# Batch 0's second half on GpSimd, batch 1's projections one matmul at a time, and another order of spills and pads

## What is computed

```python
ys = y / sqrt(128); d = rsqrt(einsum('bi,io->bo', ys * ys, w * w) + 1e-8)
xc = einsum('bsi,io->bso', x * ys[:, None, :], w) * d[:, None, :]     # modulation
q, k, v = split(xc @ w_qkv.T); q, k = rope(q), rope(k)               # 16 heads of 8
attn = softmax(where(causal, q @ k.T / sqrt(8), -inf)) @ v
x = x + attn @ w_out.T
x = x + ffn(moe(x, cond))                                             # 8 experts, 8 zones
```

## Time and profile before

| | |
|---|---|
| median of 3 runs | 181.37 us (181.26 to 181.59) |
| profiled execution: time, span | 180.98 us, 179.1 us |
| PE busy | 168.9 us (94%) |
| DVE busy | 138.9 us (78%) |
| ACT busy | 134.3 us (75%) |
| POOL busy | 93.8 us (52%) |
| share of PE in the chain that ended last | 70% |
| DMA | 24.28 MB, mean 136 GB/s |

### The profile page before, as it was taken

The page is one execution under the profiler, slowest core; times in us unless marked ns, Lnnn a source line. Parts: engine busy times, 40 slices in busy tenths (PEclk is TensorE's granted clock), DMA queues, the critical chain, the costliest instruction groups (busy, mean ns, idle before and its releaser), DMA issues.

```text
span 179.1 us, 3278 instructions
## 1 busy us (share of the span) xinstructions
PE 168.9 (94%) x943; PEld 116.8 (65%) x944; DVE 138.9 (78%) x444; ACT 134.3 (75%) x224; POOL 93.8 (52%) x117
## 2 busy tenths in 40 slices
PE   6899999899999999988999999996999989999992
PEld 2656575565666666653758767864687867788881
DVE  5588989989898899980586999699799658637551
ACT  3569177688768888889734787953879999999970
POOL 5508088985463969688532522021769931676000
PEclk9999999999999999999999999999999999999999
DMA  4824775676686567520110899960760000001001
GB/s 144 294 46 107 191 203 159 218 234 213 166 267 208 143 194 194 164 94 5 62 51 17 231 345 344 347 178 4 241 230 0 0 4 0 0 2 59 0 4 59
DMA packets 15349, 24.28 MB, mean 136 GB/s; under 512 B 2844, under 2 KB 4828, under 8 KB 15308
## 3 DMA queue, kind: packets, MB, share of 16 engines
q1 hardware_dynamic: 14532, 23.29, 42.2%
q10 hardware_dynamic: 800, 0.79, 1.7%
HBM read 18.71 MB, written 5.27 MB: 134 GB/s over the span
## 4 chain that ended last, share of the span: by engine, by line
PE 70%; DVE 11%; ACT 7%; issue 6%; POOL 4%; DVEq 0%; ACTq 0%; POOLq 0%
PE psum L1407 11%; PE psum L1540 10%; PE psum L1541 9%; PE psum L1542 9%; PE psum L1467 8%; PE psum L1443 7%; PE psum L1286 3%; PE psum L1338 2%; PE psum L1352 2%; ACT t_probs L1105 2%; DVE psum L772 2%; DVE t_raw L924 1%; PE psum L1402 1%; ACT t_q_pad L1155 1%; PE psum L1447 1%
## 5 line engine op out<-in xcount | busy, mean ns | idle before, releaser
L772 DVE CUSTOM_DVE_ANT_0 psum<-psum,t_causal 128x128 f32<-128x128 f32 (+3 forms) x128 | 58.6, 525 | 5.8 <-PE psum L1407 3.0
L1105 ACT ACTIVATE t_probs<-psum 128x1024 f32<-128x1024 f32 (+2 forms) x48 | 40.9, 883 | 8.2 <-PE psum L1443 5.2
L1407 PE MATMUL psum<-t_stacked,t_q_pad 96*128 96x256 f32 (+2 forms) x104 | 33.3, 391 | 0.5 <-DVE t_row_max L772 0.2
L1407 PEld LDWEIGHTS psum<-t_stacked,t_q_pad 96*128 96x128 f32 x104 | 18.4, 189 | 12.4 <-DVE t_row_max L772 10.2
L672 POOL TENSOR_SCALAR_AFFINE_SELECT t_probs<-t_probs 128x512 f32<-128x512 f32 x32 | 20.5, 651 | 9.0 <-ACT t_probs L1105 9.0
L944 DVE SCALAR_TENSOR_TENSOR t_q_pad<-psum,t_zw_all,t_q_pad 128x512 fp32r<-128x512 f32 x24 | 17.8, 748 | 9.3 <-ACT t_q_pad L1153 9.2
L1139 ACT ACTIVATE psum<-psum 128x512 f32<-128x512 f32 x40 | 23.4, 586 | 0.9 <-PE psum L1542 0.3
L703 POOL TENSOR_TENSOR t_q_pad<-t_raw,t_q_pad 128x512 fp32r<-128x512 f32 x8 | 10.8, 1357 | 21.0 <-ACT t_q_pad L1155 21.0
L1467 PE MATMUL psum<-t_probs,t_v_all 128*32 128x512 f32 (+3 forms) x256 | 20.6, 439 | 0.0
L772 DVE DVE_READ_ACCUMULATOR2_ANT t_row_max<- 128x1 f32 x128 | 18.0, 141 | 0.0
L1153 ACT ACTIVATE t_q_pad<-psum,t_zw_all 128x512 fp32r<-128x512 f32 x24 | 16.5, 688 | 1.2 <-PE psum L1542 0.6
(11 more groups left out here) (233 smaller groups left out, 369.6 us busy)
## 6 DMA issues: line engine op xcount, KB each, us to landing
t_stacked<-scratch SPq DMA_DIRECT2D x16, 256.0 KB, 5.7
t_probs<-in_L_ffn_Wa SPq DMA_DIRECT2D x2, 1024.0 KB, 11.5
scratch<-t_o_sb SPq DMA_DIRECT2D x7, 256.0 KB, 2.1
t_raw<-in_experts SPq DMA_DIRECT2D x7, 256.0 KB, 3.6
t_stacked<-scratch SPq DMA_DIRECT2D x9, 192.0 KB, 3.7
t_q_pad<-scratch SPq DMA_DIRECT2D x28, 48.0 KB
scratch<-t_dn_hi SPq DMA_DIRECT2D x2, 512.0 KB, 3.4
t_q_two<-scratch SPq DMA_DIRECT2D x5, 192.0 KB, 2.6
```

Source lines behind the costliest of these rows:

```text
L772: last = V.tensor_tensor_reduce(scores, scores, causal[:, S - width:S], 1.0, 3 * BIG, ALU.add, ALU.max, row_max[s][:, qb, j:j + 1])
L1105: A.activation(o, scores, ACT.Exp, scale=float(1.0 / np.sqrt(np.float32(HD)))).then_inc(exp_done, 1)
L1407: last = T.matmul(bank[:, o:o + width], q_pad[s][0:TOP, j, qb * P:(qb + 1) * P], stacked[0:TOP, n, 0:width], start=True, stop=True)
```

## The change

POOL takes over the second half's adds and remainders of batch 0 from DVE. On PE the warm-up is 5 matmuls, `modulate()` moves ahead of the second half's projections, `project` is called for one matmul at a time (`project(0, 0)` ahead of unit 0, `project(0, 1)` behind unit 2, the second stacking behind unit 3, `project(1, 0)` and `project(1, 1)` behind units 8 and 9), and fillers stand ahead of units 1, 5, 6, 7 and 11 alone. On ACT the second half's placed blocks come ahead of `copy_q0(0)`, and the spill of k right behind it. `turn(1)` on POOL stands ahead of the main loop. On SP the four pads of group 0's k stand together, behind `load_k(1)`.

```diff
-WARM = 8
+WARM = 5
...
@@ block.sync, pad_k
                     if n < BY_PE:
-                        sp.wait_ge(rep_copied, 3)
+                        sp.wait_ge(rep_copied, 2)
@@ block.sync
             spill(sp, 1, 2, 1, spilled_1)
-            sp.wait_ge(pads_zero, 1)
-            pad_k(0, (0,))
             sp.wait_ge(spilled_1[0], 16 * SPILLS)
             sp.wait_ge(q1_zero, 1)
             pad_q(1)
             sp.wait_ge(spilled_1[1], 16 * SPILLS)
             load_k(1)
-            pad_k(0, (1,))
+            sp.wait_ge(pads_zero, 1)
+            pad_k(0)
             spill(sp, 2, NG, 0, spilled)
@@ block.gpsimd
             G.memset(f32_of(k_pad[0][0:TOP]), 0.0).then_inc(pads_zero, 1)
-            pool.wait_ge(lo_ready, 4)
+            second = slice(S2, S)
+            for i in range(2):
+                pool.wait_ge(rope_ready, 3 + i)
+                G.tensor_tensor(roped[:, i, second], rope_t[i][1][:, 0, :], rope_t[i][1][:, 1, :],
+                                ALU.add).then_inc(roped_ready, 1)
+            for i in range(2):
+                pool.wait_ge(hi_ready, 3 + i)
+                G.tensor_tensor(qk_lo[:, i, second], roped[:, i, second], f32_of(qk_hi[:, i, second]),
+                                ALU.subtract).then_inc(lo_ready, 1)
             G.memset(v_all[:], 1.0).then_inc(v_ones, 1)
...
                 pool.wait_ge(pj_copied, i + 1)
-                if i == 0:
-                    pool.wait_ge(m_ready, 1)
...
             turned(0)
+            spread_last_queries(0)
+            turn(1)
...
                     if n == 0 and c == 0:
-                        turn(1)
-                    if n == 0 and c == 1:
-                        spread_last_queries(0)
                         turned(1)
@@ block.vector
-            for h in range(2):
-                if h:
-                    dve.wait_ge(ld_rotb, 16)
-                rotate(0, h)
-                rotate(1, h)
-                add_turned(0, h)
-                add_turned(1, h)
-                take_low(0, h)
-                take_low(1, h)
+            for i in range(2):
+                rotate(i, 0)
+                add_turned(i)
+            take_low(0)
+            take_low(1)
+            dve.wait_ge(ld_rotb, 16)
+            rotate(0, 1)
+            rotate(1, 1)
@@ block.scalar
             copy_k0(0)
+            place_q0(1, 0)
             take_hi_half(0, 1)
-            place_q0(1, 0)
+            place_q0(2, 0)
             take_hi_half(1, 1)
-            place_q0(2, 0)
             place_q0(3, 0)
+            place_q0(0, 1)
+            copy_k0(1)
+            for j in range(1, HG):
+                place_q0(j, 1)
             copy_q0(0)
-            copy_k0(1)
-            for j in range(HG):
-                place_q0(j, 1)
+            spill(act, 2, NG, 1, spilled)
+            copy_q0(1)
...
             copy_projection(0)
-            copy_q0(1)
             copy_v(0)
-            spill(act, 2, NG, 1, spilled)
             copy_projection(1)
@@ block.tensor, project_v
-                    pe.wait_ge(rep_copied, 2)
+                    pe.wait_ge(rep_copied, 3)
@@ block.tensor, scores_for_max
                     if u in (0, HG):
-                        pe.wait_ge(rep_copied, 3 if u else 1)
+                        pe.wait_ge(rep_copied, 2 if u else 1)
...
-                if n == 0 and u not in (0, 7):
+                if n == 0 and u in (1, 5, 6, 7, 11):
                     keep_warm(1, bank)
@@ block.tensor
             modulate_half(1)
-            for h in range(2):
-                project_half(0, h)
-                project_half(1, h)
+            keep_warm(1)
+            project_half(0, 0)
+            project_half(1, 0)
             modulate()
-            keep_warm(FILL[0])
+            project_half(0, 1)
+            project_half(1, 1)
             stack_half(0, 0)
             stack_half(1, 0)
-            project(0)
-            scores_for_max(0, 0)
+            project(0, 0)
+            for u in range(HG):
+                scores_for_max(0, u)
+                if u == 2:
+                    project(0, 1)
             stack_half(0, 1)
             stack_half(1, 1)
-            for u in range(1, len(MX_UNITS[0])):
+            for u in range(HG, len(MX_UNITS[0])):
                 scores_for_max(0, u)
                 if u == 6:
                     project_v(0)
-            project(1)
+                if u in (8, 9):
+                    project(1, u - 8)
```

More of the change, by code:

```diff
@@ L752, in rotate, with add_turned, take_low @@
                                 ALU.mult).then_inc(rope_ready, 1)
-            def add_turned(i, h):
-                dve.wait_ge(rope_ready, 2 * h + i + 1)
-                V.tensor_tensor(roped[:, i, half(h)], rope_t[i][h][:, 0, :], rope_t[i][h][:, 1, :],
+            def add_turned(i):
+                dve.wait_ge(rope_ready, i + 1)
+                V.tensor_tensor(roped[:, i, half(0)], rope_t[i][0][:, 0, :], rope_t[i][0][:, 1, :],
                                 ALU.add).then_inc(roped_ready, 1)
-            def take_low(i, h):
-                dve.wait_ge(hi_ready, 2 * h + i + 1)
-                V.tensor_tensor(qk_lo[:, i, half(h)], roped[:, i, half(h)], f32_of(qk_hi[:, i, half(h)]),
+            def take_low(i):
+                dve.wait_ge(hi_ready, i + 1)
+                V.tensor_tensor(qk_lo[:, i, half(0)], roped[:, i, half(0)], f32_of(qk_hi[:, i, half(0)]),
                                 ALU.subtract).then_inc(lo_ready, 1)
@@ L1340, in project_half, with project @@
                 last.then_inc(qk_ready, 1)
-            def project(i):
-                pe.wait_ge(xc_ready[2], 1)
-                if i == 0:
-                    pe.wait_ge(rope_ready, 2)
-                    at_ = 0
-                else:
-                    wait_slot("project", i)
-                    at_ = slot_of("project", i)
-                for t in range(2):
-                    last = T.matmul(ST[:, at_ + t, :], w_qk[:, i, t, :], xc[:, 1, :], start=True, stop=True)
-                last.then_inc(qk_ready, 1)
+            def project(i, t):
+                if t == 0:
+                    pe.wait_ge(xc_ready[2], 1)
+                    if i == 0:
+                        pe.wait_ge(rope_ready, 2)
+                    else:
+                        wait_slot("project", i)
+                T.matmul(ST[:, slot_of("project", i) + t, :], w_qk[:, i, t, :], xc[:, 1, :],
+                         start=True, stop=True).then_inc(qk_ready, 1)
             def project_v(b):
@@ L1376, in stack_half @@
                 else:
-                    pe.wait_ge(rope_ready, i + 1)
+                    pe.wait_ge(rope_ready, 3 + i)
                 bank = first_stack(i, h)
```

3 lines of the change are left out of this document (1 added, 2 removed).

## The result

The changed kernel took **182.73 us** in the median of 7 runs (182.58 to 183.10). The kernel before took 181.32 in 7 runs beside it (180.81 to 182.15). The ratio is 1.0076, with a 95% interval of 1.0061 to 1.0092: slower by 1.4 us, where 0.5 was forecast, and just outside the range (182.6). The profiled execution took 183.10 us with a span of 181.1, at the upper end of its runs.

The account below looks back on a forecast made before the run. PE is full from 34.2 to 79.3 us, so time won or lost before carries to the end. Later lay +0.6 and spread -0.1 gave +0.5 us: 181.9 beside the median of 181.37, range 180.5 to 182.6.

Parts of the forecast that it names:

- Opening: PE up to unit 0: modulate() waits for x until 8.82, unit 0 starts at 12.84, 1.0 us earlier.
- The clock rival: PE's pauses lower TensorE's clock through modulation and four projections, most of 2.64 us reaching the end: 184.0 us, chance 0.05.
- the lay: PE's matmul group laying group 0's maxima under q: forecast from 23.00 to 23.6, 0.6 us later.
- Units 4 to 7: Group 0 behind the second stacking: waits for ACT's copies lose the 1.0 us lead; DVE gets unit 7 at about 19.3.
- Units 8 to 11: End of group 0's maxima: two projection matmuls in, three fillers out; maxima ready at 23.6, 0.6 us later lay.
- POOL's adds and splits: Batch 0's second-half work moved from DVE: 0.65 us each on POOL, hidden beside PE's work, costing nothing.
- Group 0's exponentials: Behind the lay: PE's 0.51 us wait for POOL's spread goes, 0.1 us gained, bounds 0 and 0.51.
- Queues: SP's DMA order: pads of k delay the spill of q and pad_q(2); cost zero, upper bound 0.7 us.
- the rival of the late pads: The spill behind the pads makes pad_q(2) late, adding 0.5 us to the forecast: 182.4 us, chance 0.06.
- Faster: PE does not wait in units 4 to 7, unit 7 comes below 18.86: 180.7 us, chance 0.28.
- No change: Losses at units 8 to 11 half as large, PE's idle absorbs the rest: 181.4 to 181.6 us, chance 0.16.

Follow-up runs that it names:

- b2: The kernel before with five warm-up matmuls instead of eight, nothing else: 182.14 us.
- a1: The changed kernel with batch 1's x loaded ahead of the sine table and the pattern: 183.00 us.
- a2: The changed kernel with the second stacking directly behind unit 2, ahead of project(0, 1) and unit 3: 182.98 us.
- a3: The changed kernel with both matmuls of project(1) back behind unit 11: 182.50 us.
- c1: b3 with copy_q0(0) back ahead of the second half's placed blocks: 181.77 us.
- c2: c1 with project_v(0) directly behind the second stacking instead of behind unit 6: 181.71 us.
- b3: The changed kernel with eight warm-up matmuls and modulate() behind the second half's four projections: 182.14 us.
- b4: The kernel before with POOL's turn(1) and spread_last_queries(0) ahead of the main loop and turn(0) not waiting for the maxima: 181.30 us.
- d3: c2 with POOL's order of before, warm-ups split five ahead of and three behind the conditioning sum, project(1)'s matmuls behind units 8 and 11: 181.03 us.
- a4: The changed kernel with modulate() back behind the second half's four projections: 182.60 us.
- d1: The changed kernel with three more warm-up matmuls directly behind the conditioning sum: 182.64 us.
- c4: c2 with eight warm-ups split, five ahead of the conditioning sum and three behind it: 181.60 us.

## Why the prediction was right and wrong

**The step that failed is *Opening*,** which put `modulate()` at 8.82: the first projection at 5.6, three warm-ups less costed at nothing, and x's landing, read from one execution, as a fixed 5.2 us. In the profiled execution `modulate()` started at 9.86, 1.04 us later: the projection came at 7.15 and x after 6.2 us. With eight warm-ups put back the changed kernel lost 0.6 us less (182.12 in b1; 182.73). Two facts had no place in my sum. The low level can hold into the projections: 0.42 us for each instruction until 9.7 in b2, and in a1 3.12 us for eight, which ended behind x. And x's landing isn't one number: 4.9 to 6.2 us over all profiles here. The kernel before doesn't need x until 10.06, so it had 1.2 us to spare; the new place behind the first four projections has none. The clock rival's sentence "A low level before 8.8 us would be hidden behind the landing of x" held in the changed profile, where the projections ended at 9.41 and x was later still; a1 and b2 show that it need not hold, as the level was still low behind 8.8. By the a2 and a3 profiles *Opening* was right for the executions in which both go well; the changed kernel's own seven, from 182.58 up, had none such. What share of the 0.6 us is the level's and what the loads' stays open.

**What lies between unit 0 and the lay was right.** From DVE's unit 0 to the lay 10.36 us were forecast, and 10.34 were measured (10.36 in b1). *Units 4 to 7:* the lead is lost to ACT's copies, 0.78 us of DVE's idle before unit 4 and 0.91 before unit 7, and c1 and c2 show the mechanism: undoing the copy's place and v's brought unit 7 from 19.58 (b3) to 18.63. *Units 8 to 11* and the lay's release by DVE came as told. The way to unit 0 was a little short: unit 0 follows `modulate()` by 4.60 us, I had 4.42.

***POOL's adds and splits*** took 0.72 us each, estimated 0.65 (0.42 for such an add on DVE), and ended 0.37 us before the second stacking, hidden as said. No run gives them back to DVE, so what their move is worth by itself isn't measured. ***Group 0's exponentials:*** the wait is gone (34.15 shows none), and it gained nothing: from the lay to group 1's scores it is 11.21 us, 11.20 before, and b4's interval holds 1. The bounds were 0 to 0.51, and I took 0.1. ***Queues:*** zero was right for this kernel, and d3 shows that the rival of the late pads is real (1.16 us) once the lay comes earlier. Its 48 KB were called a quarter of 128 KB and are three eighths.

**The size of the order** was a little low: 0.5 forecast, and b1, with the warm-ups of before, is 0.8 slower than the kernel before (182.12; 181.35). The profiles show three parts of what is missing. The move of the lay, 0.6, was taken between two views, 23.00 of the chain and 23.6 on the timeline's clock, where the timeline has 22.84 before: 0.16 more. The way to unit 0 was 0.18 short, and the 0.1 gained at the spread did not come.

**The rivals.** *Faster* is refuted at the mark named for it: unit 7 at 20.50, and not below 18.86 in any profile with `modulate()` early (19.16 to 20.94). *No change* is outside the interval, which begins at 1.0061. *The clock* was named with 0.05, with the level low again behind a pause at 7.4 us. It isn't: behind its pause for x the changed kernel's eight projection instructions take 1.89 us, as in b2 at the high level. What some executions show is a late rise, and that deserved a term of its own with a bound: eight projection instructions at 0.42 instead of 0.22 us each, 1.6 us as in b2. The forecast had the direction at 0.55 and the sum at a third of the loss.

## What to carry to other kernels

Do not count matmuls that compute nothing, ahead of the first real one, as free to remove because a load seems to hide them. Compare the durations of one shape before and after, and do it in several executions, since the load's landing moves too. A step moved ahead to meet a load loses the slack that had absorbed the spread of that landing. And a wait that seems idle, as POOL's for the maxima, can be what keeps one engine's instruction from stretching another's on the critical path. What a reordering gains in one place must be followed to the next transfer in the queue.

## What the runs showed of the hardware

- After fewer warm-ups TensorE ran at its 1.2 GHz level up to 9.7 us in one profile (b2: 0.42 us for an instruction of 256 columns in f32, then 0.22), while the granted clock read 1.00. In a2, a3 and a4, with as few, the projections ran at the high level from 5.75 or 5.86 us on. The same kernel (b2) ran in 180.54 and in 182.86 us.
- The same load, 256 KB of x, landed 4.9 (d1) to 6.2 us (change) after its issue, with the loads ahead of it in the same order.
- A DVE cast of 128x16 took 0.53, 0.69 and 0.70 us instead of 0.18 when it began under a POOL add, and ended 0.04 us behind it (a3, c2, c4).
- POOL's add of 256 columns took 0.72 us, where 512 take 1.28.
